# Expert blocks: three of the six down products of a block in high and low parts

## What is computed

```python
T = 800; E = 8; K = 2; D = 256; H = 684
dist = sqrt(max(|x|^2 + |centroid|^2 - 2 x @ centroid.T, 1e-12))
w, sel = top_k(dist, K)
w = softmax(w)
we = zeros(T, E).at[arange(T)[:, None], sel].add(w)
for e in range(E):
    h = silu(xs @ Wg[e] + bg[e]) * (xs @ W1[e] + b1[e])
    out = out + we[:, e:e+1] * (h @ W2[e] + b2[e])
x = x + tanh(g_ffn[1]) * out
```

## Time and profile before

| | |
|---|---|
| median of 3 runs | 783.92 us (783.83 to 784.07) |
| profiled execution | 782.88 us |
| its span in the trace | 781.1 us |
| tensor engine busy | 711.4 us, 91% |
| vector, scalar, GpSimd busy | 63%, 49%, 28% |
| expert blocks of the last part | from 613.95 us on |

### The profile page before, as it was taken

How to read it: one execution, slowest core, us unless ns; L and a number is a source line. 1 busy time by engine, 2 the same in 40 slices (tenths; PEclk the granted TensorE clock), 3 DMA queues, 4 the chain that set the end, 5 groups by cost and what they waited for, 6 DMA issues and landing times.

```text
span 781.1 us, 13394 instructions
## 1 busy us (share of the span) xinstructions
PE 711.4 (91%) x4735; PEld 596.4 (76%) x4735; DVE 490.2 (63%) x956; ACT 379.0 (49%) x820; POOL 220.6 (28%) x238
## 2 busy tenths in 40 slices
PE   6999999999989699998998999998993799999996
PEld 3578888889955588577995576676773699999995
DVE  3266666665328799466657667777777465666662
ACT  4513233323362289554434466565766165656561
POOL 0006765555400043600003411114000322334232
PEclk9999999999999899998999999999996699999999
DMA  6500000000072200000000878436052388999972
GB/s 231 233 1 21 20 20 20 20 1 1 1 293 100 79 3 1 1 1 1 0 11 33 179 175 193 116 98 183 25 213 85 111 299 279 331 298 325 302 217 60
DMA packets 31441, 89.45 MB, mean 115 GB/s; under 512 B 4201, under 2 KB 20841, under 8 KB 28049
## 3 DMA queue, kind: packets, MB, share of 16 engines
q1 hardware_dynamic: 27537, 83.36, 32.9%
q0 software_dynamic: 3840, 5.25, 3.3%
HBM read 74.74 MB, written 10.38 MB: 109 GB/s over the span
## 4 chain that ended last, share of the span: by engine, by line
PE 75%; DVE 14%; ACT 4%; issue 4%; DMA 3%; POOLq 0%; SPq 0%; DVEq 0%; ACTq 0%
PE PS L514 71%; DVE SM L2124 2%; PE PS L1096 2%; PE PS L685 1%; DMA XB<-token_rows,XROW 1%; DVE RB L1879 1%; DVE SM L1791 1%; DVE RQ L1881 1%; DVE PROD L1774 1%; PE PS L1066 1%; DVE KTHL L2086 1%; PE PS L913 1%; ACT SQ L1141 1%; DVE RW L1787 1%; ACT RO L1271 1%
## 5 line engine op out<-in xcount | busy, mean ns | idle before, releaser
L514 PE MATMUL PS<-CTXH,WKV0H 128*128 128x362 f32 x256 | 86.4, 338 | 3.8 <-DVE PROD L1774 3.2
L514 PE MATMUL PS<-CTXH,WKV0L 128*128 128x362 f32 x256 | 84.0, 328 | 0.0
L514 PE MATMUL PS<-CTXL,WKV0H 128*128 128x362 f32 x256 | 84.0, 328 | 0.0
L2124 DVE TENSOR_REDUCE SM<-PS 100x1 f32<-100x362 f32 x128 | 64.5, 529 | 30.5 <-PE PS L514 29.7
L1397 ACT ACTIVATE WK<-PS 120x400 f32<-120x400 f32 (+1 forms) x96 | 48.3, 508 | 39.9 <-PE PS L514 39.2
L1813 DVE TENSOR_TENSOR RW<-PS,RW 128x400 f32<-128x400 f32 x64 | 36.8, 574 | 47.4 <-ACT RW L1207 33.7
L1207 ACT COPY RW<-PS 128x361 f32<-128x361 f32 x64 | 29.6, 463 | 65.0 <-PE PS L514 52.5
L1670 POOL DMA_INDIRECT out<-YO,TROW x20 | 33.0, 1649 | 96.8 <-DMA out<-YO,TROW 69.5
L514 PEld LDWEIGHTS PS<-CTXH,WKV0H 128*128 128x128 f32 x256 | 48.1, 188 | 12.8 <-DVE PROD L1774 6.5
L514 PE MATMUL PS<-KST,QST 97*100 97x362 f32 x128 | 51.4, 412 | 5.4 <-DVE SM L2124 4.2
L514 PE MATMUL PS<-RB,HTT 114*128 114x256 f32 (+1 forms) x240 | 55.2, 379 | 0.6 <-ACT HTT L1509 0.6
(11 more groups left out here) (326 smaller groups left out, 1813.6 us busy)
## 6 DMA issues: line engine op xcount, KB each, us to landing
RB<-W SPq DMA_DIRECT2D x14, 1368.0 KB, 6.6
RB<-W SPq DMA_DIRECT2D x20, 768.0 KB
KST<-keys_by_head SPq DMA_DIRECT2D x24, 362.0 KB
RQ<-W SPq DMA_DIRECT2D x6, 1368.0 KB
keys_by_head<-KTHL SPq DMA_DIRECT2D x8, 724.0 KB, 3.6
CTX<-ctxT SPq DMA_DIRECT2D x16, 361.0 KB, 7.0
RB<-WK SPq DMA_DIRECT2D x16, 200.0 KB, 2.2
RW<-WGU SPq DMA_DIRECT2D x1, 2304.0 KB, 8.5
```

What stands on the lines that cost most here:

```text
L514: return pe.matmul(out, lhsT, rhs, start=start, stop=stop)
L2124: dve.tensor_reduce(SM1[:, q % 2, j:j + 1], PS[0:S, i % 2, 0:KVE], AX_X, ALU.max, negate=True).then_inc(sem["c_maximum_found"], 1)
```

## The change

In the down product of each block the first three of the six pieces stay in full precision. For the last three pieces, both operands are split: the scalar engine rounds the second half of the turned hidden values into `HTH1` and three sixths of the block's `W2` into `DNH`; the vector engine makes the rests `HTL1` and `DNL`; and the tensor engine does three reduced-precision matmuls per piece, nine in place of three.

```diff
-        HTT1 = part("HTT1", [P, 6, P], "WK", 0, F32)
+        HTT1 = part("HTT1", [P, 3, P], "WK", 0, F32)
+        HTH1 = part("HTH1", [P, 3, P], "WK", 3 * P)
+        DNH = part("DNH", [P, 3, D], "RQ", GU1 + B * D + 2 * D)
+        DNL = part("DNL", [P, 3, D], "RQ", GU1)
+        HTL1 = part("HTL1", [P, 3, P], "RQ", GU1 + 3 * D)
...
@@ turn_hidden, on the tensor engine
                 if k:
                     pe.wait_ge(sem["hidden_high_ready"], N0 + 2 * k + j - 1)
+                    if j:
+                        pe.wait_ge(sem["hidden_low_ready"], N0 + k)
...
@@ down1, on the tensor engine
-                for x in range(6):
+                for x in range(3):
                     rows = HT1 if x else HT1 + 1
-                    m = mm(PS[:, 7, 0:D], HTT1[0:rows, x, :], DOWN[k % 2][0:rows, x, :], x == 0, x == 5)
+                    mm(PS[:, 7, 0:D], HTT1[0:rows, x, :], DOWN[k % 2][0:rows, x, :], x == 0, False)
+                pe.wait_ge(sem["output_weights_low_ready"], 2 + k + 1)
+                pe.wait_ge(sem["hidden_low_ready"], N0 + k + 1)
+                for x in range(3):
+                    mm(PS[:, 7, 0:D], HTH1[0:HT1, x, :], DNH[0:HT1, x, :], False, False)
+                    mm(PS[:, 7, 0:D], HTH1[0:HT1, x, :], DNL[0:HT1, x, :], False, False)
+                    m = mm(PS[:, 7, 0:D], HTL1[0:HT1, x, :], DNH[0:HT1, x, :], False, x == 2)
                 m.then_inc(sem["down_summed"], 1)
...
@@ hidden_high, on the scalar engine
-                act.copy(HTT1[0:HT1, 3 * j:3 * j + 3, :],
+                act.copy((HTT1, HTH1)[j][0:HT1, :, :],
...
+            def down_high(k):
+                act.wait_ge(sem[f"down_loaded{k % 2}"], 16 * (k // 2 + 1))
+                if k:
+                    act.wait_ge(sem["down_summed"], N0 + k)
+                act.copy(DNH[0:HT1, :, :], DOWN[k % 2][0:HT1, 3:6, :]).then_inc(sem["output_weights_high_ready"], 1)
...
@@ the block loop of the scalar engine
                 if k < NBLK:
                     hidden_high(k, 0)
+                    down_high(k)
...
@@ the vector engine
+            def down_low(k):
+                dve.wait_ge(sem["output_weights_high_ready"], 2 + k + 1)
+                dve.tensor_tensor(DNL[0:HT1, :, :], DOWN[k % 2][0:HT1, 3:6, :], DNH[0:HT1, :, :],
+                                  ALU.subtract).then_inc(sem["output_weights_low_ready"], 1)
+
+            def hidden_low1(k):
+                dve.wait_ge(sem["hidden_high_ready"], N0 + 2 * k + 2)
+                dve.tensor_tensor(HTL1[0:HT1, :, :], PS[0:HT1, 6, 0:3 * P].rearrange("p (x c) -> p x c", x=3),
+                                  HTH1[0:HT1, :, :], ALU.subtract).then_inc(sem["hidden_low_ready"], 1)
+
             for k in range(NBLK + 1):
+                if k:
+                    down_low(k - 1)
                 if k < NBLK:
                     gate_up1(k, 0)
                 if k + 1 < NBLK:
                     tokens_low(k + 1)
+                if k:
+                    hidden_low1(k - 1)
```

More of the change, by code:

```diff
@@ L269, in program @@
             a_weights_spread a_values_summed a_values_copied a_weighted a_halves_added a_heads_mixed
-            a_output_weights_high_ready a_output_weights_low_ready a_heads_high_ready
+            output_weights_high_ready output_weights_low_ready a_heads_high_ready
             a_heads_low_ready a_last_heads_low_ready a_output_summed a_output_gated a_added_to_x
@@ L595, in project_out_a @@
             def project_out_a(n, mo):
-                pe.wait_ge(sem["a_output_weights_low_ready"], 2)
+                pe.wait_ge(sem["output_weights_low_ready"], 2)
                 pe.wait_ge(sem["a_heads_low_ready"], (HB, B - 1)[n])
@@ L1223, in _ @@
                     tis = slice(b * TI0 // 2, (b + 1) * TI0 // 2)
-                    act.copy(WOUT0H[:, tis, :], WOUT0[:, tis, :]).then_inc(sem["a_output_weights_high_ready"], 1)
+                    act.copy(WOUT0H[:, tis, :], WOUT0[:, tis, :]).then_inc(sem["output_weights_high_ready"], 1)
                 round_weights(b)
@@ L1574, in _ @@
                 if b in (0, 1):
-                    pool.wait_ge(sem["a_output_weights_high_ready"], b + 1)
+                    pool.wait_ge(sem["output_weights_high_ready"], b + 1)
                     tis = slice(b * TI0 // 2, (b + 1) * TI0 // 2)
                     pool.tensor_tensor(WOUT0L[:, tis, :], WOUT0[:, tis, :], WOUT0H[:, tis, :],
-                                       ALU.subtract).then_inc(sem["a_output_weights_low_ready"], 1)
+                                       ALU.subtract).then_inc(sem["output_weights_low_ready"], 1)
                 if 1 <= b < B - 1:
```

## The result

The changed kernel takes 789.88 us (median of 3 runs, 789.58 to 790.73) against 783.92 before: 1.0082 of the time, 95% interval 1.0055 to 1.011. It is 6 us slower, 4 us above the range that I gave (780.0 to 785.9). In the profiled execution (790.73 us, span 788.9) the tensor engine does what was forecast of it, and waits for something else. First the page after the change: busy times, the shares of the chain that ended last, and the two loads with their us from issue to landing.

The account below looks back on a forecast made before the run. The tensor engine was taken to bound the expert blocks, with loads next (DMA share 0.93). -4.05 + 2.3 + 0.3 = -1.45 us took 782.88 to 781.4, or 782.5 as median; range 780.0 to 785.9.

Parts of the forecast that it names:

- the tensor engine's term: Down product: nine fp32r matmuls 0.120 us apart replace three f32 ones, 0.213 us less per block, -4.05 us over 19.
- weight-load and streaming rivals: Down-product matmul distance: 0.157 us set by loading weights (786.5 us, chance 0.05), or 0.108 by pure streaming (782.2 us, 0.07).
- the added work is hidden: Scalar and vector engines: cast 0.85, DNL 0.96, HTL1 0.56 us fit idle time, costing nothing if the cast starts on time.
- free until D = 1.9, stalls from 2.9: D, W2's landing in us into the block: later than 1.9 delays the scalar engine and GUL, from 2.9 the tensor engine.
- the landing, D = 1.7 us: W2's load lands 1.7 us into the next block: last packets at mean 1.6 in seven batches, plus 0.1.
- the term of +2.3 us for late loads: Late W2 landings in blocks 7 to 16: 1.3 for the loop, 0.6 for block 7's batch, 0.4 for scatter.
- my own loop: Late W2 delays GUL and so the next loads: two blocks take at least 6.64 + 8.9 = 15.54 us, 7.77 each.
- loads decide: slower: Rival: GUL to landing takes 9.4 us, blocks 8.02 us, total 786.1 us; chance 0.18.
- point of decision, 9.15: Time from GUL to W2's landing, in us, at about which late loads would turn the change slower.
- The signs that I set ahead: Matmuls 0.120 apart; blocks 2 to 5 at 7.64 us; in 7 to 16 casts wait for W2, XTH late, some blocks 8 us.
- the first rival (loads keep up): Rival: GUL to landing shrinks as batches meet fewer transfers, leaving -4.05 + 0.3, so 780.2 us; chance 0.25.
- The last block: Nothing hides the cast there; the last product starts 0.73 us later, booked as +0.3 us at the end.

Follow-up runs that it names:

- e3: The changed kernel with the W2 load issued ahead of the W1 load in SyncE's loop: 779.90 us, ratio to before 0.9969.
- e2: The changed kernel with DNH and DNL made from old tokens X, without the scalar engine's wait for W2 (wrong weights): 781.82 us, ratio to before 0.9968.
- e7: The changed kernel with DNH and DNL made for block 0 only and reused in all blocks (wrong weights): 781.99 us, ratio to before 0.9977.
- e10: The changed kernel run again without edit, on the chip of its W2-first version: 788.56 us, ratio to before 1.0046.
- e9: The changed kernel with W2's load issued ahead of W1's, run again beside the unedited changed kernel: 779.52 us, ratio to before 0.9927.
- e4: The kernel before the change with the W2 load issued ahead of the W1 load: 782.98 us, ratio to before 1.0005.
- e1: The kernel before the change plus the scalar engine's wait for W2 and a one-column copy at the cast's place: 786.27 us, ratio 1.0045.

## Why the prediction was wrong

**Right: the tensor engine's term.** The down product of block 11 after the change, first record and two of the nine that follow:

```profile
709.65 1.46 PE L518 MATMUL PS<-RB,HTT 115*128 115x256 f32 x6
...
711.19 0.28 PE L518 MATMUL PS<-DNH,HTL 114*128 114x256 f32 x1
...
711.90 0.28 PE L518 MATMUL PS<-DNH,HTL 114*128 114x256 f32 x1
712.02 0.49 PE L1102 MATMUL PS<-IDN,STD 128*114 128x128 f32 x3
```

From 711.19 to 711.90 are six steps: 0.118 us apart, where I had 0.120. The product takes 712.02 - 709.65 = 2.37 us, which is 1.29 + 1.08. Undisturbed blocks take 7.64 us. The formula that I took from the Trainium skill (TensorE: Matmul & The Clock Gate, section "Back-to-back issue gap") gives 109 ns here. The section calls it the isolated gap, and for streams of a weight load and a matmul it has 81 ns at 128 columns and 131 at 512. This trace agrees with neither: it has 0.118 us at 256 columns, and the 0.157 at 342 is above even the 131 ns at 512. The line through the two neighbours was nearer, though my reason for it was none: two points always lie on the line between them. The weight-load and streaming rivals fall with the 0.118.

**Right: the added work is hidden.** Durations by group (count, busy us, mean ns, idle before):

```profile
L2382 DVE TENSOR_TENSOR DNL<-RB,DNH 114x768 fp32r<-114x768 f32 x20 | 19.1, 957 | 34.1 <-ACT DNH L1540 34.0
...
L1540 ACT CAST DNH<-RB 114x768 fp32r<-114x768 f32 x20 | 16.7, 835 | 37.4 <-DMA RB<-W 37.4
...
L2387 DVE TENSOR_TENSOR HTL<-PS,HTH 114x384 fp32r<-114x384 f32 x20 | 11.0, 550 | 0.3 <-ACT HTH L1521 0.3
```

0.96, 0.84 and 0.55 us, against 0.96, 0.85 and 0.56. e3 shows that they cost nothing when `W2` is there.

**Right: where it would hurt, and by which way.** The wait at the cast, free until D = 1.9, stalls from 2.9, lateness going through XTH and GUL into the next loads (no block has a cast between 2.75 us in, which doesn't stall, and 3.51, which does; 2.9 is where the line below meets 7.64): in late blocks XTH starts 1.09 us behind the cast (I had 1.07), and a block whose cast starts later than 2.9 us in takes 4.74 us plus that start (block 8: 4.73 + 4.74 = 9.47), which is 7.64 at 2.9. Not foreseen: most of the tensor engine's idle time, 7.6 us in 8 waits, stands ahead of the down product, for HTH. I had looked at HTL1 there, and only with the cast on time. It changes no length, since GUL ends last in these blocks all the same, but the wait on GUL that I forecast hardly shows among the waits.

**Wrong: the landing, D = 1.7 us, and with it the term of +2.3 us for late loads.** The step that failed is "of such a batch the load queue's last packets are seen in 708.8 to 709.2", taken as a rule for seven batches. In block 12, the one I showed, it is right (1.9 by the count of sizes). In most others the last packets of `W2`, of 6 KB and at the very end under 512 B, come one by one for 1 to 3 us, in some while the next batch is already under way. I took the lull ahead of the next batch for the end. The landings of blocks 10 to 16 have a mean of 3.2 us, not 1.7, and GUL to landing takes 3.2 + 15.7 - 8.54 = 10.4 us, not 8.9. After the change it is 8.6 to 11.9, mean 10.1. "Landing follows the last packet closely" held: the waiter starts 0.4 to 0.6 us after the window's start, 0.2 to 0.4 after its end, where I booked 0.1. The Trainium skill (DMA: Bandwidth & Descriptors, section "Where the ~2 µs actually goes") puts most of a fixed cost of about 2 us behind the last byte. That isn't seen here either: in block 4 it is 0.7 to 0.9 us from the last 6 KB packet (648.8:649.0) to the waiter at 649.68.

With 10.4 my own loop gives (6.64 + 10.4)/2 = 8.5 us a block, and blocks 4 to 16 took 8.48 in the mean (645.04 to 755.32). Its price is 13 x (8.5 - 7.64) = 11 us, where I booked 2.3: -4.05 + 11 = +7, and block 1 to the end is 6.8 us longer. The fit to 0.2 us is partly luck: with the 10.1 measured after the change the loop gives 8.4 a block and 9 to 10 us. I also let the loop bind only from block 7 on, for 10 blocks; it bound from block 4 on. The rival "loads decide: slower" was the right one. I gave it 0.18 and priced it at 9.4; its point of decision, 9.15, lay 1.2 below what the trace of before held. (From its own terms that point should have been 9.06 for no change, and 9.3 for the 1.57 us that I called slower.)

The signs that I set ahead came out so: the casts wait, XTH is late, blocks of over 8 us are there, the matmuls are 0.118 apart. But block 4 already took 9.38 us, and I had written that blocks 2 to 5 would show a wrong 0.120 if they weren't at 7.64. That sign was badly chosen: blocks 2, 3 and 5 take 7.64 to 7.68, and block 4 is a late landing, 4.62 us in.

**Missed: no slack even at the old place.** With the loads in this order, taking the scalar engine's wait away doesn't bring the 780.2 of the first rival (loads keep up): before the change one landing came 0.1 us and one next to nothing ahead of the 4.94 at which the down product asks, in e2 a landing at 714.2 held the tensor engine up for over 1 us, and e7, with no wait on the scalar engine, has 782.0.

**The last block**, +0.3 us booked: from the start of block 19 to the end of the span it is 18.56 us before (762.54 to 781.1) and 18.31 after (770.59 to 788.9), of which one regular down product explains 0.21. The last product does start 0.73 us later, as booked: the tensor engine idles 1.35 us ahead of it, and not 0.62. But next to nothing of this reaches the end; the adds' time, which no term held, moves by as much.

**What stays open.** Why the last packets of `W2` come one at a time. They do so in batches that meet `W1` traffic and GpSimd's adds; no view here separates the DMA engines, and no run took the adds away. Nor is it shown why GUL to landing scatters from 8.6 to 11.9 us, or why it was 11.4 for block 4, the first late one. That landings alternate in blocks 4 to 10 (4.6, 1.4, 4.5, 1.2, 4.7, 1.4 and 3.8 us in) needs no further cause, though: GUL to landing is 9.5 to 10.5 in all but the first of them. A stalled block of 9.4 us puts the next landing 1.8 us earlier in its block, and its own late GUL (11.3 us in) makes the one after that late again.

## What to carry to other kernels

When a change moves the first reader of a load earlier, take the landing from something that waited for it, or from the load's own last packets, told apart by size; a lull in the queue's traffic is no landing. A load that has slack only because its reader stands late in the block can lose it with a change that shortens the block. If two loads share a queue, try the one with fewer buffers first: here two swapped statements turned +0.5% into -0.7% on one chip (e10, e9), and changed nothing in the kernel before (e4).

## What the runs showed of the hardware that was not expected

- A 768 KB load behind a 1368 KB one on the same queue can have a tail: the bulk ends, then single packets, of 6 KB and at the end under 512 B, for up to 3 us, mixed with the next load's packets (before the change up to 727.8, with the next `W1` under way from 725.6). With the small load first, issue to landing fell from 8.3 to 6.2 us.
- fp32r matmuls of 256 columns start 0.118 us apart, with `DNH` and `DNL` alternating as the streamed operand. With the full-precision records ahead of them the product takes 2.37 us; 1.29 + 9 x 0.118 is 2.35.
- The tensor engine's wait for a load can be shown as "issue", with no releaser: in e2 the load's landing (714.2) told what it was, in e7 its last packet.
- A wait can cost more than its own length: after 2.46 us of idle time in e1, and 1.85 in e10, the tensor engine's granted clock was 0.50 for about 3 us. In the first profile, with 2.15 us of idle time in block 14, it stayed at 1.00.
